# Norm 2's affine part moved out of ScalarE: its weight into w1, its bias into the rectifier

## The reference

```python
xn = _layernorm(x, axis=-1)
# six layers (i = 0..5), s starts as xn
xn1 = _layernorm(s, ln1_w[i], ln1_b[i])
q, k, v = xn1 @ wq[i], xn1 @ wk[i], xn1 @ wv[i]          # 8 heads of 16
q = softmax(q, axis=-1)          # within a head
k = softmax(k, axis=-2)          # over the 1024 tokens
attn = q @ (k^T v)               # linear attention
s = attn @ wo[i] + bo[i] + s
xn2 = _layernorm(s, ln2_w[i], ln2_b[i])
h = xn2 @ w1[i]                  # 128 -> 512
h = where(h >= 0, h, 0.01 * h)
s = h @ w2[i] + s
# side branch: top-1 of 8 experts on xn, y * its probability
out = x + s * silu(expert(xn))
```

## Time and profile before

| what | us |
|---|---|
| median of 3 runs | 596.42 |
| lowest, highest | 594.59, 596.98 |
| the profiled execution | 596.75 |
| its span, first to last instruction | 594.9 |
| PE busy | 578.7 (97% of the span) |
| DVE busy | 540.1 (91%) |
| ACT busy | 434.8 (73%) |
| POOL busy | 311.1 (52%) |

### The profile page before, as it was taken

One profiled execution on the slowest core, in us unless ns is written; L12 is line 12 of the kernel. 1 busy time (PEld: TensorE's weight loads), 2 busy tenths in 40 slices (PEclk: granted clock), 3 DMA queues, 4 the chain that ended last, 5 costly groups with the idle time before them and its releaser, 6 DMA issues.

```text
span 594.9 us, 12614 instructions
## 1 busy us (share of the span) xinstructions
PE 578.7 (97%) x4166; PEld 516.3 (87%) x4166; DVE 540.1 (91%) x1352; ACT 434.8 (73%) x763; POOL 311.1 (52%) x308
## 2 busy tenths in 40 slices
PE   7999999999999999999999999999999999999897
PEld 7899897887978889889889898898898898898796
DVE  6887999999988999999999999999999999988865
ACT  2658595876976868868768768768779678687652
POOL 5896134755852772442442532433523766867752
PEclk9989999999999999999999999999999999999999
DMA  8209233323224154445435435445342351441102
GB/s 282 75 10 328 72 110 121 124 94 130 95 84 152 71 152 146 112 133 169 124 123 163 109 141 150 116 163 158 103 165 80 108 167 57 129 156 62 45 36 106
DMA packets 74946, 73.20 MB, mean 123 GB/s; under 512 B 27265, under 2 KB 65153, under 8 KB 74882
## 3 DMA queue, kind: packets, MB, share of 16 engines
q1 hardware_dynamic: 72400, 68.18, 35.6%
q0 software_dynamic: 2048, 4.20, 2.3%
q10 hardware_dynamic: 434, 0.02, 0.0%
HBM read 39.87 MB, written 32.51 MB: 122 GB/s over the span
## 4 chain that ended last, share of the span: by engine, by line
PE 75%; DVE 11%; DMA 4%; issue 3%; POOL 3%; ACT 2%; SPq 1%; DVEq 0%; ACTq 0%; POOLq 0%
PE psY L513 23%; PE psH L406 6%; PE psS L558 6%; PE psH L407 6%; PE psH L408 6%; PE psT L592 6%; PE psT L401 6%; PE psT L526 5%; PE psM L538 5%; DVE st L1295 2%; PE psS L455 2%; DMA through<-blocks 1%; DVE X L1563 1%; DVE hid L1553 1%; DMA turned<-through 1%
## 5 line engine op out<-in xcount | busy, mean ns | idle before, releaser
L513 PE MATMUL psY<-w_all,hid 128*128 128x128 f32 x1536 | 188.7, 276 | 2.5 <-DVE hid L1553 1.8
L513 PEld LDWEIGHTS psY<-w_all,hid 128*128 128x128 f32 x1536 | 182.0, 193 | 6.6 <-issue 2.3
L1553 DVE TENSOR_TENSOR hid<-psH,hsl 128x512 f32<-128x512 f32 x192 | 127.2, 676 | 13.6 <-ACT hsl L936 13.1
L936 ACT ACTIVATE hsl<-psH 128x512 f32<-128x512 f32 x192 | 108.3, 591 | 42.0 <-PE psH L408 38.5
L2038 POOL TENSOR_TENSOR rstd<-veps,minus_half 128x8 f32<-128x8 f32 x44 | 72.7, 1653 | 61.2 <-DVE veps L1312 61.0
L2134 POOL TENSOR_TENSOR qsm<-qe,qrec 128x1024 f32<-128x1024 f32 x24 | 46.5, 1938 | 97.8 <-DVE qrec L1636 97.8
L2112 POOL TENSOR_TENSOR xn_lo<-xn,xn_hi 128x512 fp32r<-128x512 f32 x48 | 60.6, 1282 | 69.4 <-ACT xn_hi L1000 69.4
L406 PE MATMUL psH<-xn_hi,w_hi 128*128 128x512 f32 x192 | 86.4, 450 | 3.7 <-DVE hid L1553 3.4
L966 ACT ACTIVATE xh<-X,shift,rstd 128x128 f32<-128x128 f32 x188 | 77.0, 482 | 8.9 <-POOL shift L2041 8.7
L408 PE MATMUL psH<-xn_lo,w_hi 128*128 128x512 f32 x192 | 76.1, 396 | 0.0
L407 PE MATMUL psH<-xn_hi,w_lo 128*128 128x512 f32 x192 | 76.0, 396 | 0.0
(11 more groups left out here) (161 smaller groups left out, 1024.9 us busy)
## 6 DMA issues: line engine op xcount, KB each, us to landing
through<-turn SPq DMA_DIRECT2D x22, 512.0 KB, 2.7
turn<-through SPq DMA_DIRECT2D x88, 128.0 KB
through<-blocks SPq DMA_DIRECT2D x20, 512.0 KB, 3.2
turned<-through SPq DMA_DIRECT2D x80, 128.0 KB, 2.8
wb<-expert_rows SPq DMA_DIRECT2D x40, 128.0 KB, 2.0
sorted_x<-blocks SPq DMA_DIRECT2D x5, 512.0 KB, 4.4
xs_xsT<-sorted_x SPq DMA_DIRECT2D x40, 64.0 KB, 2.5
sorted_y<-ys SPq DMA_DIRECT2D x10, 256.0 KB, 2.4
```

Source lines behind the costliest of these rows:

```text
L513: last = nc.tensor.matmul(tile(psY, t), tile(hid[:, c, :], t), w2_all[:, n // NBATCH, c, :], start=(c == 0 and t == 0), stop=(c == NC - 1) ...
L936: nc.scalar.activation(hsl[:, i % 2, :], psH[:, i % 2, :], ACT.Copy, scale=SLOPE) \
L1553: nc.vector.tensor_tensor(hid[:, i % NC, :], psH[:, i % 2, :], hsl[:, i % 2, :], ALU.max) \
```

## The change

The weight of norm 2 is multiplied into w1, once per layer. The bias of norm 2, times w1, is one number for each hidden feature; it is made by small matmuls (`biases_of_hidden`: 4 of them in front, 20 later, each with one column) and added in the rectifier: `slope` now adds 0.01 times it, `leaky` adds it before it compares. `hidden_input` no longer makes the first pass: `xn2_hi` and `xn2_lo` come straight from `turned2`, read by tiles. For items 0 and 23 a plain copy from PSUM to `turned2` takes that pass's place. `turned2` is now held until `low_part` has read it, so SP waits on `xn2_lo_ready`. `split_w1` gets a second POOL operation, which scales w1 in place. The lists of all engines are written out in a new order, from the start to item 9, in the slot and at the end; SP's loads of w1, w2 and the experts change places.

```diff
@@ sync
-                    wait(sp, "xn2_ready", n)
+                    wait(sp, "xn2_lo_ready", 2 * n)
                     quadrants(turned2, through2, "turned2_ready")
...
+            gather_expert_rows()
+            feature_major2(1)
             zero_rows()
-            gather_expert_rows()
-            sp.dma_start(w1_all[:, 1:L, :], w1[1:L].rearrange("l p f -> p l f")).then_inc(sig("ffn_loaded"), 16)
-            feature_major2(1)
             feature_major2(2)
@@ tensor
+            def biases_of_hidden(lo, hi):
...
+                for l in range(lo, hi):
+                    for c in range(NC):
+                        last = nc.tensor.matmul(psS[:, l * NC + c:l * NC + c + 1],
+                                                w1_all[:, l, :].rearrange("p (m c) -> p c m", c=NC)[:, c, :],
+                                                lnp[:, 3, l:l + 1], start=True, stop=True, skip_group_check=True)
+                last.then_inc(sig("hb_done"), 1)
@@ scalar, slope
-                        nc.scalar.activation(hsl[:, i % 2, :], psH[:, i % 2, :], ACT.Copy, scale=SLOPE) \
+                        if i == 0 and n % NBATCH == 0:
+                            act.wait_ge(sig("hb_ready"), 1 if n == 0 else 2)
+                        nc.scalar.activation(hsl[:, i % 2, :], psH[:, i % 2, :], ACT.Identity,
+                                             bias=hidden_bias_sl[:, n // NBATCH, i % NC:i % NC + 1], scale=SLOPE) \
@@ scalar, hidden_input
-                wait(act, "xn2_lo_ready", 2 * n)
                 if n == 0 or n == ITEMS - 1:
+                    if n == 0:
+                        act.wait_ge(sig("sorted_rows_out"), 16)
+                    wait(act, "xn2_lo_ready", 2 * n)
                     act.wait_ge(sig("t2_done"), 1 if n == 0 else 2)
-                    nc.scalar.activation(xn2[:, :], psM[:, :], ACT.Identity, bias=param(3, n), scale=param(2, n)) \
-                        .then_inc(sig("xn2_ready"), 1)
+                    nc.scalar.activation(by_tile(turned2), natural(psM[:, :]), ACT.Copy).then_inc(sig("own2_ready"), 1)
+                    act.wait_ge(sig("own2_ready"), 1 if n == 0 else 2)
                 else:
                     act.wait_ge(sig("turned2_ready"), 16 * NQ * (turned_before2(n) + 1))
-                    nc.scalar.activation(natural(xn2[:, :]), by_tile(turned2), ACT.Identity, bias=param(3, n),
-                                         scale=param(2, n)).then_inc(sig("xn2_ready"), 1)
-                act.wait_ge(sig("xn2_ready"), n + 1)
                 wait(act, "h_done", NF * (n - 1))
-                nc.scalar.activation(parts(n)[0], xn2[:, :], ACT.Copy).then_inc(sig("xn2_hi_ready"), 1)
+                nc.scalar.activation(natural(parts(n)[0]), by_tile(turned2), ACT.Copy).then_inc(sig("xn2_hi_ready"), 1)
@@ vector
-                nc.vector.tensor_copy(w1_hi[:, :, :], w1_all[:, l, :].rearrange("p (m c) -> p c m", c=NC)) \
+                nc.vector.tensor_scalar(w1_hi[:, :, :], w1_all[:, l, :].rearrange("p (m c) -> p c m", c=NC),
+                                        lnp[:, 2, l:l + 1], None, ALU.mult) \
...
-                        nc.vector.tensor_tensor(hid[:, i % NC, :], psH[:, i % 2, :], hsl[:, i % 2, :], ALU.max) \
+                        nc.vector.scalar_tensor_tensor(hid[:, i % NC, :], psH[:, i % 2, :],
+                                                       hidden_bias[:, n // NBATCH, i % NC:i % NC + 1],
+                                                       hsl[:, i % 2, :], ALU.add, ALU.max) \
...
+            def biases_of_hidden(lo, hi):
+
+                dve.wait_ge(sig("hb_done"), 1 if lo == 0 else 2)
+                made = psS[:, lo * NC:hi * NC].rearrange("p (l c) -> p l c", c=NC)
+                nc.vector.tensor_scalar(hidden_bias_sl[:, lo:hi, :], made, SLOPE, None, ALU.mult)
+                nc.vector.tensor_copy(hidden_bias[:, lo:hi, :], made).then_inc(sig("hb_ready"), 1)
@@ gpsimd, split_w1
+                pool.wait_ge(sig("hb_done"), 1 if l == 0 else 2)
+                nc.gpsimd.tensor_tensor(w1_all[:, l, :], w1_all[:, l, :], lnp[:, 2, l:l + 1].broadcast_to([P, FF]), ALU.mult) \
+                    .then_inc(sig("w1_scaled"), 1)
+                pool.wait_ge(sig("w1_scaled"), l + 1)
@@ gpsimd, low_part
-                    nc.gpsimd.tensor_tensor(lo[:, cols], xn2[:, cols], hi[:, cols].bitcast(F32), ALU.subtract) \
+                    nc.gpsimd.tensor_tensor(natural(lo[:, cols]), by_tile(turned2)[:, 4 * half:4 * half + 4],
+                                            natural(hi[:, cols].bitcast(F32)), ALU.subtract) \
@@ gpsimd, slot
                 low_part(s - 3, 0)
+                deviations2(s - 2)
+                deviations1(s)
                 low_part(s - 3, 1)
-                deviations2(s - 2)
                 move_rows(s, 2)
                 move_rows(s, 3)
-                deviations1(s)
                 scale_queries(s - 1)
```

More of the change, by code:

```diff
@@ L552, in key_sums @@
                     wait(pe, "mix_ready", n)
+                    wait(pe, "hb_ready", 0 if n < 1 else 1 if n < 5 else 2)
                     if n < L:
@@ L616, in _ @@
             keys_by_token(0)
+            output_bias(0)
             logits(0)
             key_sums(0)
-            keys(1)
             normalised_tiles(1, 0)
             context(0)
+            keys(1)
             queries(1)
@@ L667, in _ @@
             output(0, 3)
-            output_bias(3)
+            hidden(0, 5)
+            keys(3)
             hidden(0, 6)
+            queries(3)
             hidden(0, 7)
+            hidden(1, 0)
             output(0, 4)
             output(0, 5)
+            output_bias(3)
             output(0, 6)
             output(0, 7)
-            queries(3)
+            hidden(1, 1)
             keys_by_token(3)
-            hidden(1, 0)
-            hidden(1, 1)
+            output(1, 0)
+            hidden(1, 2)
             key_sums(3)
-            hidden(1, 2)
             hidden(1, 3)
-            output(1, 0)
+            hidden(1, 4)
             output(1, 1)
             output(1, 2)
-            hidden(1, 4)
             hidden(1, 5)
@@ L772, in _ @@
             output(4, 7)
+            queries_by_feature(6)
+            hidden(5, 0)
             attention(6)
-            hidden(5, 0)
             hidden(5, 1)
@@ L777, in _ @@
             keys(7)
+            queries(7)
             hidden(5, 3)
-            queries(7)
             output(5, 0)
-            keys_by_token(7)
             hidden(5, 4)
             output(5, 1)
-            key_sums(7)
-            hidden(5, 5)
-            hidden(5, 6)
+            keys_by_token(7)
             output(5, 2)
             output(5, 3)
+            hidden(5, 5)
+            key_sums(7)
+            hidden(5, 6)
             context(7)
@@ L793, in _ @@
             attention(7)
+            output(5, 4)
             queries(8)
+            hidden(6, 0)
+            hidden(6, 1)
             keys(8)
-            output(5, 4)
             output(5, 5)
@@ L876, in _ @@
             hidden(22, 0)
+            hidden(22, 1)
             output(21, 7)
-            hidden(22, 1)
             hidden(22, 2)
+            hidden(22, 3)
             output(22, 0)
-            hidden(22, 3)
             output(22, 1)
+            hidden(22, 4)
             output(22, 2)
-            hidden(22, 4)
             hidden(22, 5)
@@ L1250, in _ @@
             norm2(22, 0)
+            slope(21, 2)
+            slope(21, 3)
+            exp_keys(23)
             norm2(22, 1)
@@ L1833, in _ @@
             query_maxima(6)
+            leaky(4, 0)
+            leaky(4, 1)
             add_y(3, 1)
```

551 lines of the change are left out of this document (277 added, 274 removed).

## The result

| | median us | lowest to highest | ratio to before, 95% interval |
|---|---|---|---|
| before | 596.38 | 594.59 to 596.98 | |
| after | 614.50 | 613.28 to 615.75 | 1.0309 [1.0277, 1.0341] |

The change makes the kernel 3.1% slower; the medians differ by 18.1 us. I had forecast 598.0 us in a range of 591.5 to 603.5: wrong, and by more than every rival allowed. The profiled execution of after took 615.75 us, with a span of 613.9 us against 594.9.

A forecast was written before the change was run, and what follows sets the result against it. TensorE, busy 578.7 of 594.9 us, was taken as the bound. Terms 0.9 + 2.2 + 1.2 + 0.4 + 0.2 - 1.3 - 2.0 - 0.3 = +1.3 us gave 598.0 us, range 591.5 to 603.5.

The forecast's parts named there:

- Bias matmuls: 24 one-column matmuls on TensorE at 0.22 us: four in front +0.9, twenty later +2.2; upper end 6.4 us for all.
- a rival with a chance of 0.04: Strided weight loads cost double: each of the 24 takes up to 0.44 us, 5.3 us above the forecast, 603.3 us.
- Half hidden in the idle time from 60 to 234 us: Twenty bias matmuls, 4.4 us, stand where TensorE idles 5.1 us waiting for VectorE; half counted as hidden, +2.2.
- The new orders: Reordered lists save time: -1.3 for POOL in slots 21 to 23, -2.0 for VectorE to item 9, -0.3 in front.
- The -1.3 for the tail: Slots 21 to 23: POOL raises norm 1's variance 4 us sooner, shortening TensorE's waits; stage idle 1.4 us, so -1.3.
- The -2.0 for VectorE from item 0 to 9: Routing lump taken apart, item 2's first rectifiers moved ahead; fills TensorE's idle time: -2.0, bounds 0 and -4.
- the -0.3 in front: POOL's eight settings of `rank` leave the first norm's path and w1's load leaves the inputs': -0.3 us.
- Rectifier: 192 on VectorE, each 54 ns longer; a third of the 3.5 us from 60 to 234 us counts: +1.2.
- The extra w1 product: One more POOL operation in `split_w1`, 1.0 us, ahead of low parts TensorE waits for: +0.2, bounds 0 and 1.5.
- SP's wait: SP waits on the low part instead of the scaled matrix: 0, at worst 2 us.
- ScalarE: 24 passes removed, copies and longer slopes added, net 10.4 us less work: worth 0, bounds -1.5 and +1.5.
- The copy of item 0: It waits for the experts' rows to be out, which start behind the loads, well before it: 0.

The follow-up runs named there:

- e2: The changed kernel without its 24 bias matmuls, the two bias tiles set to zero by VectorE: 601.88 us, 1.0098 of before.
- e1: The changed kernel with hidden features regrouped so that the bias matmuls' weight loads read side by side: 606.85 us, 1.0169 of before.
- e4: The changed kernel's orders and loads with the operations of the kernel before, no bias matmuls: 602.04 us, 1.0121 of before.
- e8: The kernel before with only the regrouped hidden features (packed weights), as a control: 599.18 us, 1.0008 of before.
- e16: The kernel before with only the changed kernel's order of SyncE's loads: 599.96 us, 1.0019 of before.
- e9: The changed kernel with VectorE's first norm moved ahead of the second input's statistics, as in before: 621.47 us, 1.0372 of before.
- e14: e2 with the plain rectifier and slope of the kernel before: 606.98 us, 1.0117 of before.
- e5: The kernel before, in its own orders, with all new operations but the bias matmuls: 621.38 us, 1.0357 of before.
- e12: e5 with the changed kernel's order of SyncE's loads, so the experts' rows are written out earlier: 610.97 us, 1.0206 of before.
- e3: The kernel before with the 24 strided bias matmuls and VectorE's four small operations added, results unread: 613.01 us, 1.0293 of before.
- e10: The changed kernel with ScalarE's two router loads put back behind the first normalised tiles: 617.76 us, 1.0303 of before.
- e6: The kernel before, in its own orders, with all new operations, bias matmuls included, weights side by side: 621.91 us, 1.0406 of before.
- e18: e3 with weights side by side: 608.31 us, 1.0165 of before.
- e7: e6 with each layer's bias matmuls behind the next output bias, four at a time, eight once: 624.82 us, 1.0408 of before.
- e15: e12 with the changed kernel's lists from slot 10 on: 608.56 us, 1.0150 of before.
- e17: e12 with VectorE's conversion of the tiles' experts moved behind the second half of the next statistics: 609.54 us, 1.0207 of before.
- e13: e12 with the plain rectifier and slope of the kernel before: 605.20 us, 1.0101 of before.

## Why the prediction was wrong, point by point

**Bias matmuls, forecast +3.1 us, measured 12.6.** This step failed most: the term was sized wrong, above all its upper end of 6.4 us. Of the 12.6 us (after to e2), 8.3 go with packed weights (after to e1) and 4.2 stay (e1 to e2). The 4.2 are the 24 x 0.22 us of the forecast; by these medians 80% of it was paid instead of 60%, a difference that the intervals don't settle. The 8.3 are the step. I took a bound of 1.21 from a GpSimd product, which reads on another engine with two inputs; a TensorE weight load took 1.7 times as long, and a matmul with its load in a row 2.1 times (0.46 us against 0.22). The rule of the Trainium skill, "SBUF — State Buffer", in its note on SBUF cachelines (a 16-byte line should be hit twice), pointed the right way. The trace agrees: 328 ns a load against 192. I had priced it as a rival with a chance of 0.04 on the one row, although that row wasn't of this engine. Even that rival (603.3) lacked the clock: while TensorE did loads and one-column matmuls for 9 us, the granted clock fell to 1.2 GHz, and behind them real work ran at half rate, an estimated 2.4 us here (8.3 less 5.9).

**Half hidden in the idle time from 60 to 234 us.** Wrong in the mechanism too. TensorE's idle time there is in short waits for VectorE at other places; under the burst of twenty in one piece VectorE ran dry instead (0.35 of 5 us busy from 145 to 150).

**The new orders, forecast -3.6 us (-1.3 - 2.0 - 0.3), measured with the old operations +7.2 (e4).** The -1.3 for the tail looks right in size (from item 20 to the end 105.4 us against 106.7), and that is luck. The power did follow its variance by 0.1 us there, but waits for `xnT` of up to 0.6 us remained, and e8 and e16 take 105.1 and 104.7 us for this stretch in the old order. What the profile of before has of its own there is a clock of 0.69 from 565 to 570 us. The -2.0 for VectorE from item 0 to 9 and the -0.3 in front had the wrong sign: in e4 3.4 us are lost by item 4 and 2.5 more by item 10. With the new operations, longer rectifier included, e2 is 5.8 us above before. I had counted idle time that an order could fill and not asked whether it did. Which of the moved lines cost the front its time isn't settled: undoing one (e9) made it worse.

**Rectifier, forecast +1.2 us.** Its length was right (736 ns, forecast 730; slope 682, forecast 681). Its price was right in the new orders (nothing to be measured) and, together with slope's 91 ns, 6 us in the old ones. The term was a property of the order, not of the instruction.

**The extra w1 product, SP's wait, ScalarE.** 1040 ns (forecast 1.0 us), no wait to be seen at either place, slots of 22.97 us. ScalarE's 11.5 us were worth nothing, as forecast: in the new orders the kernel with the pass and the one without it, both without bias, are level (e4 1.0121, e14 1.0117).

**The copy of item 0, forecast 0.** Right for the changed kernel (no wait for the experts' rows), but for the reason that its loads had been moved; without that it costs 9 us (e5 to e12). I had asked whether the write comes early enough in the new order, not what the new use of that memory adds to the old one.

## What to carry to other kernels

Before adding matmuls with one column, count their weight loads and the step in which these read: here 24 small matmuls with a 16-byte step cost 2% of the program, by the medians two thirds of it through the step, which a free choice of feature order takes away. An instruction that gets longer has no price of its own in a hand-ordered program: the same 60 ns, with 91 ns on ScalarE beside them, cost 1.0% in one order and nothing to be measured in another, so a fold and the order that suits it must be judged together. And where a bound comes from another engine's row, it isn't a bound.

## What the runs showed of the hardware

Weight loads of 128 x 128 float32 took 192 ns from packed columns and 328 ns from columns 16 bytes apart (0.22 and 0.46 us a matmul in a row). From 135 to 160 us the granted clock fell to 0.50 in all four kernels with the strided burst of twenty (after, e3, e9, e10), to 0.50 to 0.68 in the three with the packed one (e6, e1, e18), to 0.66 in e7 with eight in a row, and stayed at 1.00 in all others. In the slices with the lowest clock TensorE was busy by its records for 4.05 to 5.00 of 5 us. It falls behind waits too: 0.50 behind 5.1 us of waiting in e5. Other dips come and go and aren't explained: 0.66 at 35 to 40 us in before, which has no burst, 0.66 at 25 to 30 us in after, 0.66 to 0.70 at 175 to 180 us in e12, e15 and e17.

A conversion of 40 numbers a partition on VectorE took 3.00 us in e12 instead of 0.18, ending with two GpSimd products beside it. The Trainium skill, "SBUF — State Buffer", section "Who interferes with whom", says that a scalar operation of VectorE in a two-port mode and a GpSimd instruction exclude each other for the whole instruction. These rows agree in part: the wait ends with the second product, so VectorE was held through both, though its conversion started 0.44 us ahead of the first by the rows. That is not always so: in e1 it took 0.62 us and ended at 177.32 us, in the middle of two products (175.71 to 178.52), and in kernels with the old operations it took 0.18 us, started 0.57 us ahead of the products in before and only 0.07 us in e4, but 3.12 us in e13, started 0.57 us ahead. Why it was held in some kernels and not in others isn't shown.

Still open: what the new orders lose in front (1.0% with the new operations), and why the last slots of one kernel take a few us more in one profile than in another.
